# Cross attention and feed-forward of a decoder layer on one core: the output norm moved from the feed-forward stage into the cross-attention stage

## What is computed

```python
def _ln(x, scale, bias):                       # EPS = 1e-06
    mu = jnp.mean(x, axis=-1, keepdims=True)
    var = jnp.mean(jnp.square(x - mu), axis=-1, keepdims=True)
    return (x - mu) * jax.lax.rsqrt(var + EPS) * scale + bias
# cross attention, at its end
out = out @ Wo
return _ln(out, lno_s, lno_b)                  # scale and bias: 512 numbers each
# the layer
x = x + attention(_layernorm(x), w_qkv, w_out)                     # "x1" in the kernel
x = x + cross_attention(_layernorm(x), ctx, ..., lno_s, lno_b)     # "x2"
x = x + ffn(_layernorm(x), weight, gate_w, lora_U, lora_V)         # "x3"
```

## Time and profile before

| | us |
|---|---|
| median of 3 runs | 3515.34 |
| lowest and highest | 3514.51, 3515.39 |
| span of the profiled execution (first to last instruction) | 3511.9 |
| TensorE busy in it | 3335.3 (95%) |
| VectorE busy | 2222.4 (63%) |
| ScalarE busy | 1833.0 (52%) |
| GpSimd busy | 238.9 (7%) |

### The profile page before, as it was taken

The page is one execution under the profiler, slowest core; times in us unless marked ns, Lnnn a source line. Parts: engine busy times, 40 slices in busy tenths (PEclk is TensorE's granted clock), DMA queues, the critical chain, the costliest instruction groups (busy, mean ns, idle before and its releaser), DMA issues. The chain is left out here.

```text
span 3511.9 us, 72470 instructions
## 1 busy us (share of the span) xinstructions
PE 3335.3 (95%) x25084; PEld 2986.2 (85%) x25084; DVE 2222.4 (63%) x4888; ACT 1833.0 (52%) x4388; POOL 238.9 (7%) x324
## 2 busy tenths in 40 slices
PE   6999999998699999999999999999999999999798
PEld 6788888886488989889898898988989889899677
DVE  4666666664565756657575575755757566575487
ACT  4556555654345555555455455545555455454443
POOL 0000000000100000000000000000000000000154
PEclk8999999999799999999999999999999999999899
DMA  5554455445101001010100101101011010100133
GB/s 135 122 126 108 111 131 126 108 106 151 43 27 36 27 26 29 24 36 17 36 29 24 36 17 36 29 24 36 17 36 29 24 36 17 36 12 22 54 120 108
DMA packets 127475, 198.58 MB, mean 57 GB/s; under 512 B 18296, under 2 KB 69240, under 8 KB 126688
## 3 DMA queue, kind: packets, MB, share of 16 engines
q1 hardware_dynamic: 127200, 194.82, 21.1%
HBM read 99.35 MB, written 36.70 MB: 39 GB/s over the span
## 5 line engine op out<-in xcount | busy, mean ns | idle before, releaser
L1279 DVE CUSTOM_DVE_ANT_0 ca_prob<-ca_ps_s,ca_penalty 112x768 f32<-112x768 f32 x512 | 489.9, 957 | 532.8 <-PE ca_ps_s L1110 492.0
L1217 ACT ACTIVATE ca_probT<-ca_ps_t 128x448 f32<-128x448 f32 x512 | 277.7, 542 | 553.9 <-PE ca_ps_t L1121 550.3
L1210 ACT ACTIVATE ca_prob<-ca_prob,ca_low 112x768 f32<-112x768 f32 x512 | 476.6, 932 | 118.7 <-DVE ca_low L1279 114.7
L1095 PE MATMUL ca_ps_f<-ca_wkv_hi,ca_cnT_hi 128*128 128x256 f32 (+1 forms) x1536 | 444.4, 289 | 2.0 <-DVE ca_kstack L1322 2.0
L1095 PE MATMUL ca_ps_f<-ca_wkv_lo,ca_cnT_hi 128*128 128x256 f32 (+1 forms) x1536 | 431.9, 281 | 0.0
L1095 PE MATMUL ca_ps_f<-ca_wkv_hi,ca_cnT_lo 128*128 128x256 f32 (+1 forms) x1536 | 431.2, 281 | 0.0
L1121 PE MATMUL ca_ps_t<-ca_ident,ca_prob 112*128 112x112 f32 x3072 | 407.6, 262 | 1.5 <-ACT ca_prob L1210 0.5
L1121 PEld LDWEIGHTS ca_ps_t<-ca_ident,ca_prob 112*128 112x128 f32 x3072 | 337.4, 140 | 56.6 <-issue 29.9
L1244 ACT ACTIVATE ca_kstack<-ca_ps_f,ca_kbias 64x375 fp32r<-64x375 f32 x512 | 290.2, 567 | 180.0 <-PE ca_ps_f L1095 176.7
L1322 DVE SCALAR_TENSOR_TENSOR ca_kstack<-ca_ps_f,ca_kbias,ca_kstack 64x375 fp32r<-64x375 f32 x512 | 311.3, 608 | 99.2 <-ACT ca_kstack L1244 89.2
L1095 PE MATMUL ca_ps_f<-ca_cnT_lo,ca_wkv_hi 128*128 128x376 f32 x1024 | 342.5, 334 | 27.8 <-issue 27.8
(11 more groups left out here) (218 smaller groups left out, 7061.7 us busy)
## 6 DMA issues: line engine op xcount, KB each, us to landing
ca_q_raw<-q_T SPq DMA_DIRECT2D x128, 224.0 KB, 3.6
ca_cn<-in_ctx_dram SPq DMA_DIRECT2D x16, 1280.0 KB
sa_stack<-sa_qk_hi SPq DMA_DIRECT2D x64, 224.0 KB, 3.1
sa_stack<-sa_qk_lo SPq DMA_DIRECT2D x64, 224.0 KB, 3.5
sa_stack<-sa_qk_lo SPq DMA_DIRECT2D x128, 112.0 KB, 3.2
sa_stack<-sa_qk_hi SPq DMA_DIRECT2D x128, 112.0 KB, 3.0
q_T<-sa_q SPq DMA_DIRECT2D x16, 896.0 KB, 4.5
sa_xn<-in_x_dram SPq DMA_DIRECT2D x16, 448.0 KB, 3.6
```

The source lines that it names most:

```text
L1095: ins = nc.tensor.matmul(out, lhs[i], rhs[j], start=first_ and n == 0, stop=last_ and n == 2)
L1210: nc.scalar.activation(prob[:, h % 2, q, :], prob[:, h % 2, q, :], ACT.Exp, bias=low[:, h % 2, q:q + 1], scale=-1.0, accum_out=sums[:, h / ...
L1217: nc.scalar.activation(probT[:, h % 2, 2 * u:2 * u + 2, :], src[:, 0:2 * T].rearrange("p (k t) -> p k t", k=2), ACT.Copy).then_inc(TR.done ...
L1279: nc.vector.tensor_tensor_reduce(out=prob[:, h % 2, q, :].rearrange("p (c s) -> p c s", c=2), in0=ps_s[0:QT, :, 0:HALF], in1=penalty[:, :] ...
```

## The change

The norm is done in the cross attention by VectorE. `out` leaves ScalarE's order and comes at the end of VectorE's, followed by a new task `fin`. `out` takes mean and variance of the PSUM bank and writes (y - mean) * scale to `ca_y` with one fused operation; GpSimd takes the power -1/2; `fin` multiplies by that and adds the bias with a second fused operation. `ca_y` is now a single buffer of 112x512, stored in two DMAs per batch. Scale and bias are loaded in the set-up block. In the feed-forward the tasks `yst yag yeps yinv ysh yln ymul xb` are gone, `x2` adds `ff_y` and `ff_x1` as loaded, and the loads have four buffers and wait for `x2` of the tile four before.

```diff
         "scalar": """ ...
-            K0.0.1 T3.2.2 T3.3.0 K0.1.0 S0.0.0 R3.0 inv3.1 S0.0.1 T3.3.2 K0.1.1 Q0.1 S0.1.0 R3.1 out0 S0.1.1 out1""",
+            K0.0.1 T3.2.2 T3.3.0 K0.1.0 S0.0.0 R3.0 inv3.1 S0.0.1 T3.3.2 K0.1.1 Q0.1 S0.1.0 R3.1 S0.1.1""",
         "vector": """ ...
-            R2.1 T3.3.1 S0.0.1 inv3.1 K0.1.0 R3.0 S0.1.0 V0.1 K0.1.1 R3.1 V0.2 S0.1.1 Q0.1""",
+            R2.1 T3.3.1 S0.0.1 inv3.1 K0.1.0 R3.0 S0.1.0 V0.1 K0.1.1 R3.1 V0.2 S0.1.1 out0 Q0.1 fin0 out1 fin1""",
...
                     load_queries(sp, 0, 0)
+                    sp.dma_start(s_rows[:, :], lno_s.partition_broadcast(QT)).then_inc(rows_in, DMA)
+                    sp.dma_start(b_rows[:, :], lno_b.partition_broadcast(QT)).then_inc(rows_in, DMA)
...
                 with pool.Fori(0, TURNS) as b:
                     inverse_roots(pool, b + 1)
+                    output_roots(b)
+                output_roots(TURNS)
...
-                    sp.dma_start(y_v[bass.ds(b, 1)].rearrange("o p q d -> (o p) q d"), y_sb[:, :, :]).then_inc(y_stored, DMA)
+                    for i in range(2):
+                        sp.wait_ge(y_ready, 2 * b + i + 1)
+                        sp.sem_inc(sp_passed, 1)
+                        sp.dma_start(y_v[bass.ds(b, 1), :, i, :].rearrange("o p d -> (o p) d"), y_sb[:, :]).then_inc(y_stored, DMA)
...
+                        elif kind == "out":
+                            _, i = task
+                            n = 2 * b + i
+                            src = ps_o[O.slot(task, when)][0:QT, :]
+                            dve.wait_ge(*O.filled(task, when))
+                            moments_of(nc, dve, src, y_stats[:, i, :], y_moments[:, i, :], XLN_EPS, y_step, 2 * n, y_var, dve_passed)
+                            dve.wait_ge(y_stored, DMA * n + DMA)
+                            dve.sem_inc(dve_passed, 1)
+                            nc.vector.scalar_tensor_tensor(y_sb[:, :], src, y_moments[:, i, 0:1], s_rows[:, :], ALU.subtract,
+                                                           ALU.mult).then_inc(O.done[O.slot(task, when)], 1)
+                        elif kind == "fin":
+                            _, i = task
+                            dve.wait_ge(*O.emptied(("out", i), when))
+                            dve.sem_inc(dve_passed, 1)
+                            dve.wait_ge(y_rstd_ready, 2 * b + i + 1)
+                            nc.vector.scalar_tensor_tensor(y_sb[:, :], y_sb[:, :], y_rstd[:, i:i + 1], b_rows[:, :], ALU.mult,
+                                                           ALU.add).then_inc(y_ready, 1)
...
-        "scalar": [("gexp", 0), ("xt", 1), ("yln", 3), ("xln", 2), ("gT", 0)],
-        "vector": [("xsh", 2), ("xt", 1), ("gt", 0), ("yst", 4), ("x2", 3), ("gT", 0), ("yag", 4), ("xst", 3), ("yeps", 4),
-                   ("xag", 3), ("gmax", 1), ("xeps", 3), ("ysh", 4), ("fin", 0)],
-        "gpsimd": [("ymul", 3), ("xb", 4), ("yinv", 4), ("xinv", 3)],
+        "scalar": [("gexp", 0), ("xt", 1), ("xln", 2), ("gT", 0)],
+        "vector": [("xsh", 2), ("xt", 1), ("gt", 0), ("x2", 3), ("gT", 0), ("xst", 3), ("xag", 3), ("gmax", 1), ("xeps", 3), ("fin", 0)],
+        "gpsimd": [("xinv", 3)],
...
-                def load_next(t, p):
-                    sp.wait_ge(ys_ready, t - 1)
+                def load_next(t, n):
+                    sp.wait_ge(x2_ready, t - UNROLL + 1)
```

More of the change, by code:

```diff
@@ L782, in _, with cross_attention, feed_forward, cross_attention_stage @@
                 all_turns(dve, parts["vector"] | {"first": [t for t in others if t[0] not in ("st", "ln")]}, run, later_weights)
-def cross_attention(nc, context, mask, null_kv, q_T, y, shared, kv_raw, kv_in, o_raw, o_in, s_col, b_col, ln_in, load_next_weights):
+handed = {}
+def cross_attention(*args):
+    handed["cross"] = args
+def feed_forward(nc, x1, y, lno_s, lno_b, w_raw, u_raw, g_raw, v_raw, w_in, w_loads, out):
+    cross_attention_stage(lno_s, lno_b, *handed["cross"])
+    feed_forward_stage(nc, x1, y, w_raw, u_raw, g_raw, v_raw, w_in, w_loads, out)
+def cross_attention_stage(lno_s, lno_b, nc, context, mask, null_kv, q_T, y, shared, kv_raw, kv_in, o_raw, o_in, s_col, b_col, ln_in,
+                          load_next_weights):
     B, KEYS, D = context.shape
@@ L1087, in _ @@
                 load_next_weights(sp)
-                store(TURNS, ("last", TURNS))
-                sp.wait_ge(y_stored, DMA * B + DMA)
+                store(TURNS)
+                sp.wait_ge(y_stored, 2 * DMA * B + DMA)
             @block.tensor
@@ L1251, in run @@
                             nc.scalar.activation(q_part[0][:, 2 * i:2 * i + 2, :], q_raw[:, 2 * i:2 * i + 2, :], ACT.Copy).then_inc(q_hi, 1)
-                        elif kind == "out":
-                            _, i = task
-                            if i == 0:
-                                act.wait_ge(y_stored, DMA * b + DMA)
-                            act.wait_ge(*O.filled(task, when))
-                            nc.scalar.activation(y_sb[:, i, :], ps_o[O.slot(task, when)][0:QT, :], ACT.Copy).then_inc(O.done[O.slot(task, when)], 1)
-                act.sem_inc(y_stored, DMA)
                 act.wait_ge(fixed_ready, 6)
@@ L1351, in _ @@
                         dve.sem_inc(d, 1)
+                dve.sem_inc(y_stored, DMA)
+                dve.wait_ge(rows_in, 2 * DMA)
                 dve.wait_ge(fixed_ready, 6)
@@ L1464, in _, with run @@
                 make_constants(nc, pool, ident, minus_half, ident_ready)
-                pool.wait_ge(rows_in, 2 * DMA)
-                def run(task, t, half, v):
+                def run(task, t, half, v, turn):
                     p = v % 2
-                    if task == "xb":
-                        pool.wait_ge(y_in[p], 2 * DMA * half + 2 * DMA)
-                        nc.gpsimd.tensor_tensor(xb[:, p, :], x1_sb[:, p, :], b_rows[:, :], ALU.add).then_inc(xb_ready, 1)
-                    elif task == "yinv":
-                        inverse_root(nc, pool, y_rstd[:, :], moments[:, 0, 1:2], minus_half[:, :], y_var, t, y_rstd_ready)
-                    elif task == "ymul":
-                        pool.wait_ge(yn_ready, t + 1)
-                        nc.gpsimd.tensor_tensor(ys[:, :], yn[:, :], s_rows[:, :], ALU.mult).then_inc(ys_ready, 1)
-                    elif task == "xinv":
-                        inverse_root(nc, pool, x_rstd[:, p:p + 1], moments[:, 1, 1:2], minus_half[:, :], x_var, t, x_rstd_ready)
+                    if task == "xinv":
+                        inverse_root(nc, pool, x_rstd[:, p:p + 1], moments[:, 1:2], minus_half[:, :], x_var, t, x_rstd_ready)
                 all_turns(pool, table["gpsimd"], run)
@@ L1496, in store @@
                     sp.dma_start(rows[2][bass.ds(t, 1)].rearrange("o p d -> (o p) d"), x3[:, p, :]).then_inc(out_stored[p], DMA)
-                load(0, 0)
-                load(1, 1)
-                sp.dma_start(s_rows[:, :], lno_s.partition_broadcast(P)).then_inc(rows_in, DMA)
-                sp.dma_start(b_rows[:, :], lno_b.partition_broadcast(P)).then_inc(rows_in, DMA)
-                AHEAD = LEAD + 2
-                for t in range(2, AHEAD):
-                    load_next(t, t % 2)
-                with sp.Fori(0, (TILES - AHEAD) // 2) as j:
-                    for p in range(2):
-                        load_next(2 * j + p + AHEAD, p)
-                        store(2 * j + p, p)
-                for t in range(TILES - AHEAD, TILES):
+                for t in range(UNROLL):
+                    load(t, t)
+                with sp.Fori(0, TILES // UNROLL - 1) as j:
+                    for n in range(UNROLL):
+                        load_next(UNROLL * j + UNROLL + n, n)
+                        store(UNROLL * j + n, n % 2)
+                for t in range(TILES - UNROLL, TILES):
                     store(t, t % 2)
```

88 lines of the change are left out of this document (33 added, 55 removed).

## The result

The changed kernel takes 3537.72 us (median of 4 runs, 3536.60 to 3544.49), beside 3515.36 us for the kernel before (4 runs, 3514.51 to 3517.07). The ratio is 1.0069, 95% interval 1.0057 to 1.0081: **slower by 22 us (0.7%)**, where 3490.7 was predicted. The span of its profiled execution is 24.2 us longer than that of the earlier trace rows.

A forecast was written before the change was run, and what follows sets the result against it. TensorE was taken to bound the cross attention, a closed chain through GpSimd and VectorE the feed-forward step. Terms -18.8 - 7.9 + 2.05 = -24.65 gave a span of 3487.25, plus 3.44 is 3490.7 us; 8-in-10 range 3486 to 3501.

The forecast's parts named there:

- The bound of the cross attention: Cross attention: TensorE, busy 98.5%, sets the time; other engines' work costs nothing until TensorE waits for it.
- the feed-forward: Feed-forward: steps fall from 6.159 to TensorE's 5.34 us, gaining 18.8 us; the first tile gains 7.9 us more.
- no wait of `lora`: Feed-forward, a sign of success: TensorE's `lora` no longer waits for `ff_gT_lo`, where it waited 0.58 us a step.
- the first tile: Feed-forward start: `x2` of tile 0 starts right after VectorE's set-up, so `ug` comes earlier, gaining 7.9 us.
- End of the stage: Cross attention's last batch: no work covers `out1`, so the end comes 2.05 us later, keeping 3.2 for the store.
- End of a turn, "the cost is nothing": Cross attention, turn's end: VectorE's added 4.9 us a turn is covered by its idle time, costing TensorE nothing.
- The spare of 1.18 us: Cross attention, next turn's start: score ends at 3042.1, slot needed at 3043.28; the prediction called it 1.1 us left.
- the store's landing: Cross attention rival: the single buffer's slow store stalls TensorE; a 5.0 us landing costs 10.5 us, 3501.2; chance 0.10.
- VectorE's first instructions come late: Cross attention rival: a 2.0 us wait behind VectorE's branch makes the score 0.8 late, 12 us, 3502.7; chance 0.05.
- slower than before: Cross attention rival: store landing passes 5.9 us; at 6.5 it costs 33 us, ending at 3523.7; chance 0.03.
- The argument against the fetch: Cross attention: VectorE's loop has a sixth of TensorE's instructions, and its other loops show no such wait.
- the move of the query loads: Cross attention, turn's end: SyncE's query loads move from 3031.59 to 3033.35 and take 1.30 us to issue.

The follow-up runs named there:

- e1: Kernel before with the changed kernel's feed-forward and no output norm at all (result isn't the layer's): 3492.09 us, ratio 0.9928.
- e11: Changed kernel with the turn's last query loads issued behind both stores of `y` on SyncE: 3513.03 us, ratio 0.9994 to the kernel before.
- e2: Changed kernel with the last query split `Q0.1` ahead of `out0` in VectorE's order: 3528.18 us, ratio 1.0031 to the kernel before.
- e3: Changed kernel with a second buffer for `y`, placed in `ca_rsum`: 3504.63 us, ratio 0.9967 to the kernel before.
- e8: Kernel before with five idle reductions of 1100 columns at VectorE's end of a turn, making it 6.1 us late: 3532.93 us, ratio 1.0038.
- e5: Changed kernel, but ScalarE copies the banks as before and VectorE does each batch's norm in the next turn's idle times: 3506.33 us, ratio 0.9967 to before.
- e10: e5 with query loads behind ScalarE's two copies and turn 0's zeros written later by GpSimd: 3483.39 us, ratio 0.9909 to the kernel before.

## Why the prediction was wrong

**The bound of the cross attention, and the feed-forward: right.** 5.39 us a step (5.34), 6.3 us to `ug` of tile 0 (6.6), no wait of `lora`; 26.7 us gained by the stage, 26.4 by e1, where the sum had 18.8 + 7.9. That the sum is met to a tenth is partly luck, as the steps came 0.05 us longer and the first tile 0.3 shorter than forecast.

**End of the stage: right mechanism, too large.** +1.3 us where the sum had 2.05. The store of half the size lands sooner. By the Trainium skill (DMA: Bandwidth & Descriptors, section on the anatomy of one DMA, which describes DMAs issued by GpSimd) the estimate for 224 KB was 2.5 us. The two stores of the last batch, issued by SyncE, took 2.3, so here the page was nearer than the 3.2 of the larger store that I kept.

**End of a turn, "the cost is nothing": this step failed.** I let the score end 7.35 us behind TensorE's branch, with 1.18 us to the point where its slot is needed. It ended at 11.45. (Between the turn's last score and the next turn's first copy stand eleven arithmetic instructions of VectorE, not the ten of the section on the change.) Part by part, from the boundary at 1420.90:

| us behind TensorE's branch | predicted | measured | added |
|---|---|---|---|
| store of `out0` landed | 3.15 | 4.3 | 1.15 |
| from there to the end of `fin1` | 1.4 | 1.72 | 0.3 |
| VectorE's fetch behind its branch | 0 | 2.45 | 2.45 |
| from the first copy to the end of the score | 2.8 | 2.96 | 0.2 |
| score ends | 7.35 | 11.45 | 4.1 |

The spare of 1.18 us taken off, 2.9 are left, which is the 3.0 us that TensorE's score starts late, and nearly the 3.18 of a turn. The landing took 4.1 us on average (3.2 in the sum). With the query loads moved away it still takes 3.4 (e11) and 3.7 (e2), so they account for less than half of what is above 2.3; the rest goes with the instruction packet. The fused operation measured 0.75 us, not 0.69, and `fin` waited 0.22 more for it.

**The rivals.** Two of them were what happened, "the store's landing" and "VectorE's first instructions come late", and I had priced each alone against the whole spare: the landing at 4.2 would have cost nothing, the fetch 0.8 to 1.3 us. Together they cost 3. They lie on one chain, one behind the other, so their latenesses add and the spare is there once. As exclusive cases with 0.10 and 0.05 they hid the case that came true, and the range couldn't hold it. The rival "slower than before" asked one term alone for a landing of 5.9 us, where the sum of three small ones did it.

The argument against the fetch was wrong too. I said that VectorE's other loops show no such wait, and that is so: in the self attention and the feed-forward its next instruction comes 0.14 to 0.29 us behind the branch. But the cross attention's own loop had the wait already before the change, 3.1 to 3.4 us in each of 14 turns. It lay under the idle time of the earlier trace rows, where the first copy came only at 3035.70, and the trace of the kernel before had it. VectorE's branch and the next instruction of its sequencer, before and after:

```profile
L1361 DVEq COMPARE_BRANCH  x1: 68/68/68, 3030.1 to 3030.1; - x1
L1361 DVEq FUSED_REGOPS  x1: 62/62/62, 3033.6 to 3033.6; - x1
```

```profile
L1399 DVEq COMPARE_BRANCH  x1: 68/68/68, 1426.3 to 1426.3; - x1
L1399 DVEq FUSED_REGOPS  x1: 63/63/63, 1429.3 to 1429.3; - x1
```

The fetch is no longer than before (2.7 to 3.0 us in the 14 turns). What the change did to VectorE's branch is to move it from 4.7 us ahead of TensorE's branch to 5.4 behind it, and to take away what covered the fetch.

**Not thought of at all:** the move of the query loads was charged with its 1.3 us of issue, not with what their bytes do to TensorE's fetch. In the changed kernel itself this costs little, since TensorE would wait for the score anyway; in e3 it is most of the 0.8 us a turn left. The low clock is alike where it falls ahead of the wait for the score: e8's turns take 148.5 us without and 148.7 with it, as the slower TensorE uses up its own waiting. Where it falls behind that wait, it is paid. That happened in 2 of the changed kernel's 14 turns, which took 152.1 and 152.3 us against 150.1 to 150.9 in the others.

**Still open:** how often the clock falls. It isn't the stall's length alone: in e3 a stall of 3.12 us kept the upper level, and one of 2.17 lost it. And what made e5's stall longer than before the change. Its query loads are issued where they were and land 1.3 us behind the branch (1.7 before). What its trace does show moved is the load of the mask, issued 1.1 us ahead of the branch on average, where it had been 1.9 behind; that it is the cause wasn't tested. e10 makes two edits at once, and the mask's load moves with them, to 2.9 us behind; the turn's gain is read from the stall, the set-up's from the first branch (from 238.9 to 236.0 us behind the last store of the queries).

## What to carry to other kernels

Add up all the lateness that a change puts on one chain, and take the spare off once; rivals that share a chain aren't alternatives. Look whether an engine's loop has a fetch of instructions behind its branch, even one that costs nothing yet. Where it has, as VectorE's here in the cross attention, the end of the turn is an expensive place for an instruction that waits for a semaphore: the fetch of the next turn then stands in the open, and everything behind the branch is late by that much. Not every loop has it. In the feed-forward after the change VectorE's last instruction of a turn waits too, and the next one follows at once:

```profile
3447.45 0.69 DVE L1658 TENSOR_TENSOR ff_x<-ff_ps_b,ff_x 128x512 f32<-128x512 f32 x1 [0.31 <-PE ff_ps_b L1534]
3448.05 0.20 DVE L1636 TENSOR_SCALAR ff_x_shift<-ff_moments,ff_x_rstd 128x1 f32<-128x1 f32 x1
```

When the same arithmetic is done a turn later in the idle times of the loop, and the loads are kept out of the time in which the busiest engine passes its branch, the move that lost 22 us gains 31.
